# Two attention layers, experts and an LSTM in one pipelined kernel: one chain of addends, wide reciprocals, new orders

## The reference

```python
x = x + attention0(layernorm(x), ctx)   # 16 heads of 8, softmax, 64 keys, biases
x = x + experts(layernorm(x))           # 8 experts, the top 2 by gate score
x = x + attention1(layernorm(x), ctx)   # 16 heads of 8, no biases
x = x + h(layernorm(x))                 # a gated recurrence over the 128 steps, below

# experts: scores = x @ W_gate + b_gate; w = the two highest scores at their places, else 0
# out = sum over e of w[e] * (relu(x @ W1[e] + b1[e]) @ W2[e] + b2[e])
# recurrence: f, i = sigmoid(x wf + c uf + bf), sigmoid(x wi + c ui + bi)
#             c = f * c + i * tanh(x wc + c uc + bc);  h = tanh(x wo + c_final uo + bo)
```

## Time and profile before

| | us |
|---|---|
| median of 3 runs (980.33 to 986.9) | 980.34 |
| the profiled execution, its own time | 981.66 |
| its span, first to last instruction | 979.7 |

### The profile page before, as it was taken

How to read it: one execution, slowest core, us unless ns; L and a number is a source line. 1 busy time by engine, 2 the same in 40 slices (tenths; PEclk the granted TensorE clock), 3 DMA queues, 4 the chain that set the end, 5 groups by cost and what they waited for, 6 DMA issues and landing times.

```text
span 979.7 us, 37648 instructions
## 1 busy us (share of the span) xinstructions
PE 859.3 (88%) x13267; PEld 763.5 (78%) x13267; DVE 843.1 (86%) x2878; ACT 820.0 (84%) x2650; POOL 618.8 (63%) x1026
## 2 busy tenths in 40 slices
PE   2778889999999999999999999999999999988750
PEld 1467778888888888888888888888888888877540
DVE  0377899999999999999999999999999999988638
ACT  2467789999999999999999999999999999877633
POOL 2455666676766676766676766676766676754415
PEclk9689999999999999999999999999999999999975
DMA  6920000000000000000000000000000000000006
GB/s 134 250 58 2 2 3 3 3 4 3 2 3 3 3 3 3 3 3 3 3 3 3 2 3 3 3 3 3 3 3 2 4 3 3 3 2 2 2 1 171
DMA packets 37991, 17.34 MB, mean 18 GB/s; under 512 B 9176, under 2 KB 37792, under 8 KB 37808
## 3 DMA queue, kind: packets, MB, share of 16 engines
q1 hardware_dynamic: 37248, 14.67, 5.9%
q0 software_dynamic: 128, 0.07, 0.1%
q10 hardware_dynamic: 432, 0.21, 0.1%
HBM read 10.74 MB, written 4.19 MB: 15 GB/s over the span
## 4 chain that ended last, share of the span: by engine, by line
DVE 60%; PE 20%; issue 12%; ACT 3%; SPq 2%; DVEq 1%; POOL 1%; DMA 0%; ACTq 0%; POOLq 0%
DVE acc L961 13%; DVE mx L827 11%; DVE Ex L841 11%; PE ps L395 4%; PE ps L349 3%; DVE x L965 3%; PE ps L360 3%; PE ps L301 3%; DVE AB L975 3%; DVE x L888 2%; DVE mv L813 2%; PE ps L439 2%; DVE st L786 2%; DVE CG L978 2%; PE ps L461 2%
## 5 line engine op out<-in xcount | busy, mean ns | idle before, releaser
L1092 POOL TENSOR_TENSOR h<-Ex 128x512 f32<-128x512 f32 (+1 forms) x140 | 165.6, 1183 | 155.0 <-issue 135.8
L827 DVE TENSOR_REDUCE mx<-ps 128x8 f32<-128x512 f32 (+1 forms) x280 | 166.1, 635 | 30.5 <-PE ps L334 30.5
L636 ACT ACTIVATE ET<-ps 128x512 f32<-128x512 f32 (+1 forms) x280 | 160.5, 573 | 10.3 <-PE ps L349 10.0
L841 DVE TENSOR_TENSOR Ex<-ps,mx 128x512 f32<-128x512 f32 (+1 forms) x280 | 165.6, 630 | 0.0
L349 PE MATMUL ps<-cst,Ex 128*128 128x128 f32 x1024 | 150.1, 276 | 4.8 <-ACT kv L564 2.1
L625 ACT ACTIVATE Ex<-Ex 128x512 f32<-128x512 f32 (+1 forms) x280 | 152.5, 611 | 0.0
L1076 POOL TENSOR_TENSOR rs<-ve,half 128x4 f32<-128x4 f32 (+3 forms) x74 | 69.1, 934 | 119.9 <-DVE ve L817 119.9
L677 ACT ACTIVATE hT<-ps,col 128x128 f32<-128x128 f32 x512 | 137.2, 371 | 0.0
L439 PE MATMUL ps<-w,hT 128*128 128x128 f32 x1024 | 131.6, 283 | 0.0
L349 PEld LDWEIGHTS ps<-cst,Ex 128*128 128x128 f32 x1024 | 119.3, 143 | 9.6 <-ACT kv L564 4.4
L418 PE MATMUL ps<-xT,w 128*128 128x128 f32 x1024 | 125.4, 276 | 0.0
(11 more groups left out here) (111 smaller groups left out, 1951.2 us busy)
## 6 DMA issues: line engine op xcount, KB each, us to landing
out_dram<-x SPq DMA_DIRECT2D x15, 256.0 KB, 2.5
x<-in_x_dram SPq DMA_DIRECT2D x7, 512.0 KB, 7.0
cx<-in_ctx_dram SPq DMA_DIRECT2D x7, 512.0 KB, 6.8
w<-in_L_ffn_W_dram SPq DMA_DIRECT2D x2, 512.0 KB, 5.1
x<-in_x_dram SPq DMA_DIRECT2D x1, 256.0 KB, 3.0
cx<-in_ctx_dram SPq DMA_DIRECT2D x1, 256.0 KB, 3.3
out_dram<-x SPq DMA_DIRECT2D x2, 128.0 KB, 2.2
b<-in_L_ffn_b_dram SPq DMA_DIRECT2D x9, 4.0 KB
```

The lines of the kernel that those rows point to most:

```text
L636: e.activation(ET[:, j % 2, r, lo:hi, :, :], b[:, 256 * lo:256 * hi].rearrange("p (c w q) -> p c w q", c=hi - lo, w=2), ACT.Copy).then_inc ...
L827: e.tensor_reduce(mx[:, j % 2, r, 4 * lo:4 * hi], b[:, 256 * lo:256 * hi].rearrange("p (j k) -> p j k", k=64), AX.X, ALU.max).then_inc(sig ...
L841: e.tensor_tensor(Ex[:, j % 2, r, 256 * lo:256 * hi].rearrange("p (j k) -> p j k", k=64), b[:, 256 * lo:256 * hi].rearrange("p (j k) -> p ...
L1092: e.tensor_tensor(u, v[:, :, :, 0:32], v[:, :, :, 32:64], ALU.add).then_inc(sig("half1"), 1)
```

## The change

- Offsets 5, 9 and 14, 81 slots, new LAG, new orders on all engines, and USES in the new order with a step and a first count for each reader (a bank of the experts is now given back in the middle of the chain).
- `inverse` takes the reciprocal of the sums read as a broadcast and writes rd, 128 x 128 for each side. `widen` is gone.
- `combine` is nine calls: c0 adds the bias product in PSUM to x, c1 to c8 are multiply-adds on one accumulator, the last of which writes x. ScalarE's `expert_bias` and the closing sum are gone.
- `gate_sum` moves to GpSimd.
- Weight groups 1 to 3 are turned in slots FIRST + 6 to FIRST + 8.
- At the end TensorE forms half of the sums (identity times cx, plus identity times the cell's part), VectorE the other half and all of the closing sums; GpSimd has none.

```diff
-TAIL = [("dve", 4), ("pool", 4), ("dve", 4), ("dve", 4), ("pool", 4), ("dve", 4),
...
+TAIL = [("dve", 4), ("pe", 4)] * 7 + [("dve", 4), ("pe", 2), ("dve", 2)]
+EARLY = 2
-L1, L2, L3 = 4, 6, 10
+L1, L2, L3 = 5, 9, 14
-FIRST, LAST = -1, NT + 12
+FIRST, LAST = -1, NT + 16
...
 # tensor_program, the loop and behind it
-                if FIRST + 2 <= i < FIRST + 5:
-                    turn_weights(i - FIRST - 1)
+                if FIRST + 6 <= i < FIRST + 9:
+                    turn_weights(i - FIRST - 5)
+                query(i)
+                turn_e(i, 3)
+                turn_r(i)
+                scores(i)
+                step(i, 1)
+                turn_e(i, 2)
+                experts(i, 0)
+                cell_inputs(i)
+                keys_values(i)
+                step(i, 0)
+                values(i)
+                turn_x(i)
+                turn_e(i, 0)
+                experts(i, 1)
+                turn_e(i, 1)
+                ctx_turn(i)
+                turn_w(i)
+                hidden(i, 1)
+                gate(i)
+                hidden(i, 0)
+                project(i)
+                expert_bias(i)
+                out_inputs(i)
...
+            def share(k, part):
+                lo, n = mine[k]
+                src = cx[:, lo:lo + n, :] if part == 0 else cU[:, :].unsqueeze(1).to_broadcast([P, n, 128])
+                return e.matmul(banks[k % 7][:, 0:128 * n], ident, src, start=(part == 0), stop=(part == 1),
+                                skip_group_check=True)
+
+            for _, reader, _, chain, step, first in USES:
+                e.wait_ge(sig(reader), step * (SPAN[chain][1] - 1) + first)
+            for k in range(EARLY):
+                share(k, 0)
             e.wait_ge(sig("C"), 2 * NT + 1)
...
+            e.wait_ge(sig("cU"), 1)
+            for k in range(len(mine)):
+                if k >= EARLY:
...
+                    share(k, 0)
+                share(k, 1).then_inc(sig("pre_pe"), 1)
 # vector_program
                 e.wait_ge(sig("sm"), j + 1)
                 if j >= 2:
-                    e.wait_ge(sig("rd"), j - 1)
-                e.reciprocal(ri[:, j % 2, :, 4 * lo:4 * hi], sm[:, j % 2, :, 4 * lo:4 * hi]).then_inc(sig("ri"), 1)
+                    e.wait_ge(sig("rt"), j - 1)
+                for c in range(lo, hi):
+                    m = e.reciprocal(rd[:, j % 2, c, :].rearrange("p (r h d) -> p r h d", r=4, d=8),
+                                     sm[:, j % 2, :, 4 * c:4 * c + 4].unsqueeze(3).to_broadcast([P, 4, 4, 8]))
+                m.then_inc(sig("rd"), 1)
...
+            def combine(i, n):
+                t = i - LAG[f"c{n}"] - L1
+                if not on(t):
+                    return
+                d = acc[:, t % 2, :]
+                if n == 0:
+                    b = bank_of("yb", t + L1)
+                    e.wait_ge(sig("yb"), t + 1)
+                    e.tensor_tensor(d, b[:, 0:128], x[:, t, :], ALU.add).then_inc(sig("acc"), 1)
+                    return
...
+                e.wait_ge(sig("acc"), 8 * t + n)
+                m = e.scalar_tensor_tensor(x[:, t, :] if n == 8 else d, b[:, 128 * k:128 * k + 128],
+                                           we[:, t % 2, n - 1:n], d, ALU.mult, ALU.add)
+                m.then_inc(sig("xm" if n == 8 else "acc"), 1)
...
 # its new order
+                combine(i, 8)
+                sums(i)
+                stats_inputs(i)
+                update(i, 0)
+                gate(i)
+                inverse(i)
+                project(i)
+                combine(i, 0)
+                gate_float(i)
+                stats_attention(i)
+                stats_experts(i)
+                gate_weights(i)
+                gate_top(i)
+                spread(i)
                 maxima(i, 2)
                 maxima(i, 0)
                 maxima(i, 1)
-                gate_sum(i)
                 differences(i, 0)
+                update(i, 1)
+                differences(i, 1)
+                maxima(i, 3)
                 differences(i, 2)
...
                 differences(i, 3)
+                combine(i, 1)
+                combine(i, 2)
+                combine(i, 3)
+                combine(i, 4)
                 normal(i)
+                combine(i, 5)
+                combine(i, 6)
+                combine(i, 7)
                 gate_index(i)
 # its end
+            share(mine.pop(0))
+            share(mine.pop(0))
+            for k in range(len(TAIL)):
+                e.wait_ge(sig("tanh"), k + 1)
+                e.tensor_tensor(x[:, lo[k]:lo[k + 1], :], cx[:, lo[k]:lo[k + 1], :], x[:, lo[k]:lo[k + 1], :],
+                                ALU.add).then_inc(sig("out"), 1)
+                if mine and k % 2 == 0:
+                    share(mine.pop(0))
 # gpsimd_program, its new order
+                keys(i, 0)
+                spread_values(i)
+                spread(i)
+                gate_sum(i)
+                halves(i, 1)
+                gate_pieces(i)
                 halves(i, 0)
...
+                keys(i, 1)
                 add_bias(i)
```

More of the change, by code:

```diff
@@ L221, in sync_program @@
                 load_c(c)
[L222 to L225, removed]
+            lo = 0
+            for k, (_, n) in enumerate(TAIL):
+                e.wait_ge(sig("out"), k + 1)
                 e.dma_start(o_v[:, lo:lo + n, :], x[:, lo:lo + n, :]).then_inc(sig("stored"), 16)
@@ L237, in bank @@
                 while v >= len(USES) * FIRST:
-                    _, reader, lag, chain, times = USES[v % len(USES)]
+                    _, reader, lag, chain, step, first = USES[v % len(USES)]
                     n = v // len(USES) - lag - SPAN[chain][0]
@@ L241, in bank @@
                         if reader not in done:
-                            e.wait_ge(sig(reader), times * (n + 1))
+                            e.wait_ge(sig(reader), step * n + first)
                         break
@@ L494, in tensor_program @@
                     project_bias()
-                if FIRST + 2 <= i < FIRST + 5:
-                    turn_weights(i - FIRST - 1)
[L497 to L516, removed]
+                if FIRST + 6 <= i < FIRST + 9:
+                    turn_weights(i - FIRST - 5)
                 query(i)
                 turn_e(i, 3)
-                turn_e(i, 1)
+                turn_r(i)
[10 more added lines that the diff above has]
+                experts(i, 1)
+                turn_e(i, 1)
+                ctx_turn(i)
[6 more added lines that the diff above has]
+                out_inputs(i)
+            mine, lo = [], 0
+            for adder, n in TAIL:
+                if adder == "pe":
+                    mine.append((lo, n))
+                lo += n
+            def share(k, part):
[7 more added lines that the diff above has]
+                share(k, 0)
             e.wait_ge(sig("C"), 2 * NT + 1)
@@ L524, in tensor_program @@
                      skip_group_check=True).then_inc(sig("uo"), 1)
+            e.wait_ge(sig("cU"), 1)
+            for k in range(len(mine)):
+                if k >= EARLY:
+                    if k >= 7:
+                        e.wait_ge(sig("tanh"), [n for n, (adder, _) in enumerate(TAIL) if adder == "pe"][k - 7] + 1)
+                    share(k, 0)
+                share(k, 1).then_inc(sig("pre_pe"), 1)
         def scalar_program(e):
@@ L738, in scalar_program @@
                     e.wait_ge(sig("cell"), 1)
+                query(i)
                 turn_e(i, 3)
-                query(i)
+                exps(i, 2)
+                turn_r(i)
                 gates(i, 1)
+                exps(i, 1)
+                exps(i, 0)
+                turn_e(i, 2)
+                scale(i)
+                gates(i, 0)
+                keys_values(i)
+                turn_x(i)
+                exps(i, 3)
+                turn_e(i, 0)
+                ctx_turn(i)
                 turn_e(i, 1)
-                widen(i)
-                keys_values(i)
-                scale(i)
+                turn_w(i)
+                relus(i, 1)
                 relus(i, 0)
[L747 to L755, removed]
-                out_inputs(i)
[L757 to L761, removed]
+                out_inputs(i)
+            lo, begun = 0, {"dve": 0, "pe": 0}
             for adder, n in TAIL:
+                e.wait_ge(sig("pre_" + adder), begun[adder] + 1)
+                src = cx[:, lo:lo + n, :]
+                if adder == "pe":
+                    src = banks[begun[adder] % 7][:, 0:128 * n].rearrange("p (t d) -> p t d", t=n)
                 begun[adder] += 1
-                e.wait_ge(sig("pre_" + adder), begun[adder])
-                e.activation(cx[:, lo:lo + n, :], cx[:, lo:lo + n, :], ACT.Tanh).then_inc(sig("tanh_" + adder), 1)
+                e.activation(cx[:, lo:lo + n, :], src, ACT.Tanh).then_inc(sig("tanh"), 1)
                 lo += n
@@ L1013, in vector_program @@
                 maxima(i, 1)
-                gate_sum(i)
                 differences(i, 0)
```

(39 more changed lines are left out.)

111 lines of the change are left out of this document (17 added, 94 removed), and 29 rows, old and new, of tables (LAG, USES).

## The result

The changed kernel takes 996.5 us (995.98 to 998.43, 4 runs) against 980.7 before: ratio 1.0158, 95% interval 1.0115 to 1.02. It is slower by about half of what was forecast (1010), and inside the range. The changed kernel's profiled execution has a span of 994.0 us against 979.7.

What follows compares the result with a forecast made beforehand. VectorE's instructions and the short gaps between dependent ones were taken to set the slot. 50 full slots x 14.1 (705) + start and drain 285 + tail 19.5 = 1009.5 us of span, forecast 1010, range 966 to 1042.

Steps and rivals of the forecast that it cites:

- The rival of a cheap wide reciprocal: Wide reciprocal on VectorE costs little, so the change is faster; TensorE's floor then holds the slot: 951 us; chance 0.11.
- the one of a dearer one: Each reciprocal element on VectorE costs 8.3 ns instead of 6.1, by a repeat count of 8: 1046 us; chance 0.12.
- the free chain: On VectorE's one accumulator, a dependent multiply-add costs no more than a free one: 38 us less, 972; chance 0.13.
- the stalls in front of L875 and L888: VectorE's idle 0.41 us before L875 and 0.15 before L888 in each full slot go with the new order.
- the slow clock feared there: In the tail TensorE might run at half clock, 26 us for its products; a few slow microseconds were taken, 15.5.
- The term for new meetings with GpSimd: VectorE's two-input SBUF operations may be held by GpSimd in each slot: 0.3 us added, bounds 0 and +0.9.
- the gate's run: VectorE's six dependent gate operations now stand apart, estimated to save 0.2 us of stalls per slot.
- one of my own signs of being wrong: Wrong if the reciprocal is about 0.3 us, a slot under 13.5, or start and drain together far from 285.
- I keep all that idle time and add the work: Start and drain: part-filled slots keep their idle time, and four full slots' work is added: 232.1 + 4 x 12.5 = 282.
- the 10.80 of the row: TensorE's wait in its second slot for the last of nine weights, 10.80 us; later weight turns were credited -11.
- TensorE's floor near 13.2: TensorE's 12.83 us of work per slot plus 0.4 of waits would keep a slot from going below 13.2.
- below about 5 ns per element: Reciprocal price at which the cheap rival decides: the slot comes down to 13.8 us and the sum to 980.

Runs made afterwards that it cites:

- the one undone without moving anything: Changed kernel with the 128x32 reciprocal again, widened by two copies on VectorE itself, no call moved: 940.8 us, ratio 0.957 to the kernel before.
- the run without the early products: Changed kernel without the tail's two TensorE products in front of the last LSTM product (EARLY = 0): 997.0 us, ratio 1.0146 to the kernel before.
- the run with VectorE's copies: Changed kernel with the narrow 128x32 reciprocal, widened by two VectorE copies, no call moved: 940.8 us, slot 13.35.

## Why the prediction was right, and where its sizes were off

The wide reciprocals are a cause, as forecast. A wide one was priced from two shapes at 920 ns; the trace has 921 on average over 128, and the one undone without moving anything gives the 55 us back. The rival of a cheap wide reciprocal is out, and so is the one of a dearer one, as is the free chain: dependent multiply-adds are 0.38 apart, as said. VectorE's queue bound the slot, and the stalls in front of L875 and L888 went as said. The tail was put at 19.5 and is 19.2; the slow clock feared there did not come, and the run without the early products shows that it was these that kept it off.

The sign, slower, did not follow from the reciprocals alone. It also took the held update, for which the sum had only 0.3 us: with the update moved off GpSimd's halves, and the wide reciprocals kept, the kernel takes 963.7 us. With a hold of 0.3 us instead of 0.87 an estimate from these runs is 994.0 - 50 x 0.57 = 965.5 us of span, faster than before and at the lower end of the range (966 to 1042). That the kernel came out slower is in part luck: the hold cost more than the sum had for it, and start and drain, below, cost less.

These two terms were mis-sized.

- The slot: 14.06 forecast, 14.30 measured. The term for new meetings with GpSimd was 0.3 out of 0 to 0.9; it is 0.87, shown by taking it away (0.73 came back). So the slot should have been 14.6; the other 0.3 is spread over small terms, by the spacings in the two slots: the stall before `normal` gave 0.08 more than said, the gate's run 0.07, the reciprocals and `project` 0.06 each. The chain came out as added up: 2.78 before, 2.88 after. The sum used 14.1, so 50 slots make +10 us (+12 by 14.06).
- Start and drain: 285 forecast, 974.8 - 50 x 14.3 = 260 measured, below my bound of 265, and far from 285 was one of my own signs of being wrong. The step that failed is "I keep all that idle time and add the work". The work term was about right (VectorE 73 us more busy there, 64 forecast; my windows hold about one slot more than the forecast's start and drain). The idle time is 42 us less and not 11. 16.5 of it hangs on the weight turns, shown by undoing them, where I took the 10.80 of the row; the removal of a wait is worth what it would be in the new schedule, not in the old. The other 25 us or so I put down to the longer lags, under which a part-filled slot has fewer waits of one engine for another inside itself. That is argued, not shown: no kernel here has the old lags with the rest new.

The sum of it: 994.0 instead of 1009.5, of which the edges are -25, the slots +10 and the tail -0.3.

"TensorE's floor near 13.2" in the prediction, by which the cheap rival was priced, was wrong as well: TensorE allows a slot of 12.62. Had the reciprocal been cheap, the kernel would still have been held by GpSimd at 13.35, as the run with VectorE's copies shows; that the rival's price (951) lies near this run's 941 is luck. Nor does the mark "below about 5 ns per element" add up: 50 x 13.8 + 285 + 19.5 is 994.5, not 980, and by the sum's own terms the mark lies near 4 ns.

## What to carry to other kernels

Price a wider operation from two of its own shapes before it is moved to the busiest engine: here the reciprocal that looked like a saved hand-over was 6 ns an element, and a narrow one with plain copies behind it does the same in 0.66 us of the queue instead of 1.67. In a schedule that is full, where each engine works through its list in order, a move is worth what is saved at that place less what it lets come late; four of the edits tried here took work or a stall out of VectorE's queue and got next to nothing or a loss, two brought 30 us or more, and only the timeline of all engines in one slot tells which it will be. When VectorE takes two inputs from SBUF, look at what GpSimd does in that microsecond.

## What the runs showed of the hardware

- A reciprocal costs about 6.1 ns per element on VectorE: 238, 335 and 921 ns for 16, 32 and 128 elements lie on one line.
- A VectorE operation with two SBUF inputs is held while GpSimd's halves (128x512 and 128x256) run beside it, until they end: 0.23 us became 1.19, 0.28 became 0.60. Unheld ones of the same line stand in the same slot. Beside GpSimd's power on 128x4, 1.02 us long, L978 kept its 0.23. With GpSimd idle the tail's 128x512 sums all take 0.68, where 9 of 20 took 1.75 before.
- Two fp32 copies of 128x128 in SBUF cost VectorE's queue 0.28 us together, from 504.16 to 504.44; GpSimd was idle there.
